# The opening of a two-layer model on one core: tokenizer bias as a product row, row copies on two engines, the first norm scaled on VectorE, a quarter turned inside the loop, constants loaded earlier

## The reference

```python
for i in range(9):                                  # tokenizer: dilated causal convolutions
    h = relu(conv1d(x, conv_w[i], dilation=2**i) + conv_b[i])
    x = x + h * scale[i] + shift[i]                 # batch norm folded into scale and shift
y = conv1d(x, out_w, 0, 1) + out_b                  # 4 -> 64 channels, one tap
h = transpose(y)                                    # (B, L, D)
xn = layernorm(h)                                   # no gain, no bias
q = einsum('btd,hrd->bhtr', xn, Q); k = einsum('bud,hrd->bhur', xn, K)   # 8 heads of rank 32
attn = softmax(q @ k.T / sqrt(64)); h = h + sum_h((attn @ xn) @ VO[h])
# then: a routed FFN of 8 experts, a second attention of another kind, a second FFN of 6 experts
```

## Time and profile before

| | us |
|---|---|
| median of 3 runs | 1347.37 |
| lowest and highest | 1346.24, 1347.96 |
| the profiled execution, its own time | 1345.62 |
| its span, first to last instruction | 1343.6 |

### The profile page before, as it was taken

The page is one execution under the profiler, slowest core; times in us unless marked ns, Lnnn a source line. Parts: engine busy times, 40 slices in busy tenths (PEclk is TensorE's granted clock), DMA queues, the critical chain, the costliest instruction groups (busy, mean ns, idle before and its releaser), DMA issues.

```text
span 1343.6 us, 27026 instructions
## 1 busy us (share of the span) xinstructions
PE 1228.2 (91%) x10203; PEld 785.8 (58%) x10203; DVE 780.1 (58%) x1724; ACT 641.1 (48%) x1372; POOL 526.5 (39%) x1110
## 2 busy tenths in 40 slices
PE   6889999999999999999999998699718888889998
PEld 5755565665666666666666665455415676676553
DVE  3545555665556566566566562142677898984542
ACT  1325555555554554554545544050245754744564
POOL 3211454754554644555455444405880120421200
PEclk8969999999999999999999999699858677568999
DMA  4100000000000000000000001012110000000001
GB/s 84 18 5 2 2 3 2 4 6 2 3 3 2 3 3 2 2 2 2 3 2 3 2 3 33 5 75 61 18 16 0 1 1 0 13 1 1 13 12 23
DMA packets 34076, 14.57 MB, mean 11 GB/s; under 512 B 30738, under 2 KB 31346, under 8 KB 33949
## 3 DMA queue, kind: packets, MB, share of 16 engines
q1 hardware_dynamic: 29341, 10.95, 3.6%
q0 software_dynamic: 4608, 1.91, 1.6%
HBM read 6.46 MB, written 7.27 MB: 10 GB/s over the span
## 4 chain that ended last, share of the span: by engine, by line
PE 73%; DVE 11%; POOL 5%; issue 5%; ACT 4%; SPq 2%; DMA 1%; POOLq 0%; DVEq 0%; ACTq 0%
PE psum L755 21%; PE psum L736 10%; PE psum L664 8%; PE psum L727 8%; PE psum L711 4%; POOL XN L1310 3%; PE psum L1008 2%; PE psum L649 2%; DVE arena L1978 2%; PE psum L558 2%; PE psum L988 1%; PE psum L669 1%; PE psum L809 1%; PE psum L822 1%; PE psum L1023 1%
## 5 line engine op out<-in xcount | busy, mean ns | idle before, releaser
L1428 ACT ACTIVATE arena<-psum 125x500 f32<-125x500 f32 x576 | 306.9, 585 | 337.7 <-PE psum L736 337.7
L1779 DVE TENSOR_REDUCE arena<-psum 125x1 f32<-125x500 f32 x384 | 242.4, 673 | 201.7 <-PE psum L664 201.7
L664 PE MATMUL psum<-arena 32*125 32x500 f32 (+1 forms) x1536 | 323.3, 517 | 0.6 <-ACT arena L1419 0.6
L755 PE MATMUL psum<-arena,XN 125*64 125x250 f32 x2304 | 307.9, 388 | 0.2 <-ACT arena L1428 0.2
L736 PE MATMUL psum<-arena 32*125 32x250 f32 x2304 | 291.7, 370 | 0.0
L736 PEld LDWEIGHTS psum<-arena 32*125 32x125 f32 x2304 | 214.6, 183 | 11.8 <-issue 1.0
L755 PEld LDWEIGHTS psum<-arena,XN 125*64 125x64 f32 x2304 | 140.3, 136 | 121.3 <-issue 78.6
L1782 DVE TENSOR_REDUCE arena<-psum 125x2 f32<-125x500 f32 x192 | 121.2, 673 | 71.7 <-PE psum L664 67.5
L664 PEld LDWEIGHTS psum<-arena 32*125 32x125 f32 x1536 | 126.8, 183 | 4.2 <-ACT arena L1419 1.2
L727 PE MATMUL psum<-arena,onesb 3*125 3x500 bf16 x576 | 122.4, 422 | 1.4 <-DMA arena<-arena 1.4
L1204 POOL TENSOR_TENSOR lnst<-lnst,mhalf 125x12 f32<-125x12 f32 x14 | 32.0, 2286 | 227.6 <-DVE lnst L1758 227.6
(11 more groups left out here) (342 smaller groups left out, 1970.9 us busy)
## 6 DMA issues: line engine op xcount, KB each, us to landing
arena<-arena SPq DMA_DIRECT2D x192, 1.5 KB
expert_in<-XN SPq DMA_DIRECT2D x8, 256.0 KB, 4.8
arena<-expert_in SPq DMA_DIRECT2D x4, 512.0 KB, 4.9
expert_out<-arena SPq DMA_DIRECT2D x4, 512.0 KB, 2.8
out<-H SPq DMA_DIRECT2D x16, 93.8 KB
expert_in<-XN,slot_in POOLq DMA_INDIRECT x48
XN<-expert_out,slot_out POOLq DMA_INDIRECT x48, 3.3
arena<-in_L_ffn_w SPq DMA_DIRECT2D x2, 256.0 KB
```

The source lines that it names most:

```text
L664: last = pe.matmul(ps[0:R, at_:at_ + hi - lo], QH[row:row + 32, b, g, j * R:(j + 1) * R], KH[row:row + 32, b, g, lo:hi], start=True, stop= ...
L755: last = pe.matmul(ctx_bank[64 * h2:64 * h2 + 64, 0:THIRD], XN[:, p, c, a, :], PR[:, x % 4, h2, i * THIRD:(i + 1) * THIRD], start=(c == 0) ...
L1428: act.activation(PR[:, x % 4, h2, :], st_bank[(2 * x + h2) % 3][0:R, 0:2 * THIRD], ACT.Exp)\
L1779: dve.reduce_max(MX[:, q % 2, 0, 2 * h2 + tile:2 * h2 + tile + 1], ps[0:R, 0:2 * THIRD], AX)\
```

## The change

- The output bias becomes row 96 of the product's weight, `Wout1`, loaded by a DMA that writes it 24 times into one partition; row 96 of `xc1` is set to 1 by GpSimd. The products have 97 rows.
- The six products are copied to `H` in one instruction each, the even ones by VectorE and the odd ones by ScalarE. ScalarE's two sines go behind its squares.
- VectorE clears `Fw`, as its first instruction. SP issues `prep` ahead of the eight zeroing DMAs; the `zeroed` counts are exchanged accordingly and `zeros` is cleared last.
- In the first norm GpSimd does the power alone, and VectorE the multiplication. VectorE's order is sum and centring of quarter 0, sum of quarter 1, variance 0, centring 1, variance 1, both scalings.
- Only quarter 0 is turned ahead of the attention. Quarter 1 becomes two ring jobs `("xt", 0, 1, h)` in steps 3 and 4, copied by VectorE; its `values_ready` follows them.
- The eight projections ahead of the loop go by halves of the rows; ScalarE copies Q, VectorE copies K.
- `busy`: 24 ahead of block 0 in place of 8; one after each score of `before`, and six after that list.

```diff
-        Wout, at = view(at, [NS * B, D], parts=96)
+        Wout1, at = view(at, [NS * B, D], parts=97)
+        Wout = Wout1[0:96]
...
-        xc, at = view(at, [SEG], parts=96)
+        xc1, at = view(at, [SEG], parts=97)
+        xc = xc1[0:96]
...
+            if x in (3, 4):
+                found.append(("xt", 0, 1, x - 3))
...
-        before = [job + (a,) for job in projections(0, 0) for a in range(2)]
+        before = [("proj", 0, 0, qk, th, a) for th in range(2) for qk in range(2) for a in range(2)]
...
+        halves = [(half, s) for half in range(2) for s in range(NS)]
...
-                busy(ps, 4 if i else 8)
+                busy(ps, 4 if i else 24)
...
-                    pe.matmul(ps[0:R, :], xc[:, half * R:(half + 1) * R], Wout[:, 8 * s:8 * s + 8, :],
+                    pe.matmul(ps[0:R, :], xc1[:, half * R:(half + 1) * R], Wout1[:, 8 * s:8 * s + 8, :],
...
-            for p in range(2):
-                transposes(0, xn_tile, p, S["normed0"], 6 if p else 34)
+            transposes(0, xn_tile, 0, S["normed0"], 34)
...
-                    if a == 0 and p >= 2:
-                        ring_emptied(pe, ("xt", 1, p, 0))
-                        ring_emptied(pe, ("xt", 1, p, 1))
+                    if a == 0 and p:
+                        for h in range(2):
+                            ring_emptied(pe, ("xt", int(p >= 2), p, h))
...
+                    if k_ == 0:
+                        pe.wait_ge(S["normed0"], 2)
...
-            ring_in(before)
+            for job in before:
+                ring(job)
+                if job[0] == "score":
+                    busy(st_bank[0], 1)
+            busy(st_bank[0], 6)
...
-            sp.dma_start(outb[:, :], t["L0_tok_out_b"].partition_broadcast(R)).then_inc(S["dma_conv"], 16)
+            sp.dma_start(Wout1[96:97], t["L0_tok_out_b"].unsqueeze(0).unsqueeze(0).to_broadcast([1, NS * B, D]))\
+                .then_inc(S["dma_conv"], 16)
 
             sp.wait_ge(S["zeroed"], 1)
+            for dst, src in prep:
+                sp.dma_start(dst, src).then_inc(S["dma_prep"], 16)
+            sp.wait_ge(S["zeroed"], 2)
             for e in range(E0):
...
-            sp.wait_ge(S["zeroed"], 2)
-            for dst, src in prep:
-                sp.dma_start(dst, src).then_inc(S["dma_prep"], 16)
...
+            pool.memset(xc1[96:97], 1.0)
...
-            pool.memset(Fw, 0.0)
...
-            scale(0, 0)
-            scale(0, 1)
+            for p in range(2):
+                pool.wait_ge(S["variance0"], p + 1)
+                pool.tensor_tensor(lnst[:, 3, p, :], lnst[:, 2, p, :], mhalf[0:R, 0:2 * NJ], ALU.pow)\
+                    .then_inc(S["rstd0"], 1)
...
+            for n, (half, s) in enumerate(halves):
+                if n % 2:
+                    ps, done = filled(act, ("h0", half, s))
+                    act.activation(H[:, :, 2 * s + half].rearrange("r p a d -> r a p d"),
+                                   ps[0:R, :].rearrange("r (a p d) -> r a p d", a=2, p=NP), ACT.Copy).then_inc(done, 1)
...
             for job in before:
-                if job[0] == "proj":
+                if job[0] == "proj" and job[3] == 0:
                     projected(job)
...
+            link(dve.memset(Fw, 0.0))
...
+                if n % 2 == 0:
                     ps, done = filled(dve, ("h0", half, s))
...
+                    dve.tensor_copy(H[:, :, 2 * s + half].rearrange("r p a d -> r a p d"),
+                                    ps[0:R, :].rearrange("r (a p d) -> r a p d", a=2, p=NP)).then_inc(done, 1)
...
+            def first_scale(p):
+                dve.wait_ge(S["rstd0"], p + 1)
+                dve.tensor_tensor(pairs(XN, p), pairs(XN, p), over(lnst[:, 3, p, :], 2 * NJ, D), ALU.mult)\
+                   .then_inc(S["normed0"], 1)
+
+            first_sum(0)
             dve.wait_ge(S["xbuf_zero"], 16 * E0)
...
+            first_centre(0)
+            first_sum(1)
+            variance(0, 0)
+            first_centre(1)
+            variance(0, 1)
+            first_scale(0)
+            first_scale(1)
...
+            for job in before:
+                if job[0] == "proj" and job[3] == 1:
+                    _, p, g, qk, th, a = job
+                    k = ring_at[job]
+                    dve.wait_ge(S["ring_full"], k + 1)
+                    dve.tensor_copy(KH[:, p + NP * a, g, th * HALF:(th + 1) * HALF], ring_bank[k % RB][:, 0:HALF])\
+                       .then_inc(ring_free[k % RB], 1)
```

More of the change, by code:

```diff
@@ L124, in build @@
         ppt, at = view(at, [NJ * R], parts=PP)
-        outb, at = view(at, [D], parts=R)
         phases, at = view(at, [NJ * PP + WN], parts=R)
@@ L249, in build @@
         sem(*[f"{what}{k}" for k in range(4) for what in ("centred", "squared", "variance", "normed")])
-        sem("dve_chain", "act_chain", "pool_chain")
+        sem("dve_chain", "act_chain", "pool_chain", "rstd0")
         sem("zeroed", "dma_conv", "dma_weights", "consts", "w96", "conv_w", "bn_var", "bn_rstd",
@@ L673, in ring @@
                     p = b % NP
-                    pe.wait_ge(S["lnb_done"], ln_at[(k_, b + NP if k_ == 1 else b)] + 1)
+                    if k_ == 0:
+                        pe.wait_ge(S["normed0"], 2)
+                    else:
+                        pe.wait_ge(S["lnb_done"], ln_at[(k_, b + NP if k_ == 1 else b)] + 1)
                     for i in range(3):
@@ L1181, in _ @@
             pool.memset(wearly, 0.0)
-            pool.memset(zeros, 0.0).then_inc(S["zeroed"], 1)
             pool.memset(qload, 0.0)
@@ L1185, in _ @@
             pool.memset(vox[:, :, :], 0.0).then_inc(S["zeroed"], 1)
+            pool.memset(zeros, 0.0).then_inc(S["zeroed"], 1)
             pool.wait_ge(S["consts"], 2)
@@ L1218, in _ @@
             link(pool.memset(SO[:, NJ, :], 0.0))
[L1219 to L1222, removed]
+            for h in range(2):
+                pool.wait_ge(full[jobs[("xt", 0, 0, h)] % 8], jobs[("xt", 0, 0, h)] // 8 + 1)
+            values_ready(0)
             for job in order:
@@ L1237, in _ @@
                     pool.tensor_scalar(nm[:, :, 2, :], rb, -1.0, None, ALU.mult).then_inc(S["shift_in"], 1)
-                elif kind == "xt" and job[1] == 1 and job[3] == 1:
+                elif kind == "xt" and job[1] < 2 and job[3] == 1:
                     pool.wait_ge(S["ring_full"], ring_at[job] + 1)
@@ L1360, in _ @@
                             ps, done = filled(act, ("qkp", qk, a))
-                            act.wait_ge(S["zeroed"], 2)
+                            act.wait_ge(S["zeroed"], 1)
                             act.activation(qkp[:, a, qk, :], ps[:, 0:256], ACT.Copy).then_inc(done, 1)
@@ L1409, in _ @@
             squares(0, 1, xn_flat(1))
+            act.wait_ge(S["trig_r"], 1)
+            act.activation(trig[:, 1, :], phases, ACT.Sin).then_inc(S["trig_done"], 1)
+            act.activation(trig[:, 0, :], trig[:, 0, :], ACT.Sin, bias=halfpi[0:R, :], scale=-1.0)\
+               .then_inc(S["trig_done"], 1)
             to_xt(0, 0)
-            to_xt(0, 1)
             def projected(job):
@@ L1735, in _ @@
                     dve.scalar_tensor_tensor(x1, x0, -1.0, x0, ALU.mult, ALU.max).then_inc(S["trig_r"], 1)
-            for half in range(2):
-                for s in range(NS):
+            for n, (half, s) in enumerate(halves):
+                if n % 2 == 0:
                     ps, done = filled(dve, ("h0", half, s))
[L1739 to L1745, removed]
+                    dve.tensor_copy(H[:, :, 2 * s + half].rearrange("r p a d -> r a p d"),
+                                    ps[0:R, :].rearrange("r (a p d) -> r a p d", a=2, p=NP)).then_inc(done, 1)
+            for half, s in halves:
+                emptied(dve, ("h0", half, s))
             def centre(k, p, src, dst):
@@ L1759, in variance, with first_sum, first_centre @@
                    .then_inc(S[f"variance{k}"], 1)
-            dve.wait_ge(S["xbuf_zero"], 16 * E0)
[L1762 to L1765, removed]
+            def first_sum(p):
+                link(dve.reduce_sum(lnst[:, 0, p, :], pairs(H, p), AX))
+                link(dve.tensor_scalar(lnst[:, 1, p, :], lnst[:, 0, p, :], -1.0 / D, None, ALU.mult))
+            def first_centre(p):
+                dve.tensor_tensor(pairs(XN, p), pairs(H, p), over(lnst[:, 1, p, :], 2 * NJ, D), ALU.add)\
+                   .then_inc(S["centred0"], 1)
+            def first_scale(p):
[3 more added lines that the diff above has]
+            first_sum(0)
+            dve.wait_ge(S["xbuf_zero"], 16 * E0)
+            first_centre(0)
[12 more added lines that the diff above has]
+                       .then_inc(ring_free[k % RB], 1)
             for job in order:
@@ L1796, in _ @@
                     p, a = b % NP, b // NP
-                    r = slice(0, 128) if which == 1 else slice(64 * a, 64 * a + 64)
+                    r = slice(0, 128) if which < 2 else slice(64 * a, 64 * a + 64)
```

## The result

The changed kernel takes 1355.7 us (median of six runs, 1354.9 to 1361.7) against 1347.7 before (six runs, 1346.2 to 1349.5): a ratio of 1.0071, 95% interval 1.0049 to 1.0092. It is slower by 0.7%, where 1335.7 was forecast with 1330.5 to 1344.0. Its profiled execution took 1355.9 (span 1353.6), 10.0 longer in the span than the one before.

The account below looks back on a forecast made before the run. The prediction took TensorE to bound the loop and one serial chain, with low clock in dense work, to bound what precedes it. Its terms summed to -11.7 us: 1335.7 against the median 1347.4, range 1330.5 to 1344.

Parts of the forecast that it names:

- Part 7: First score to loop: fillers part the paired scores, 1.1 us per score, 14.8 us instead of 10.30, +4.5.
- The clock falls in the scores: Rival: scores with filler take 2.2 us each at low clock, steps 0 to 2 their old 16.8; 1352, chance 0.15.
- Parts 1 and 2: Convolution blocks: longer filler starts block 0 at 16.4 us (+1.8); faster blocks, earlier constants, output product at 44.5 (-4.4).
- Part 3: Output product: bias as a row and copies split over two engines, -0.2 us.
- part 4: First norm, up to the first transposes: scaling on VectorE instead of GpSimd, -0.95 us.
- Part 5: First transposes to projections: the second quarter's turn no longer stands ahead of the projections, -3.8 us.
- Part 6: Projections to first score: full clock, K copied by VectorE beside ScalarE's Q, 3.4 us, -1.7.
- Part 9: Loop steps 3 and 4: six transposes enter where TensorE has no slack, +0.9 us.
- Part 8: Loop steps 0 to 2: 10.7 us instead of 16.8, -6.1, if the clock stays up.

Follow-up runs that it names:

- e4: Changed kernel with three fillers after each score instead of one; four runs 1349.3, 1349.6, 1369.1 and 1369.1 us, ratio 1.0111 to the kernel before.
- e3: Changed kernel with a filler after every second score only, the six behind the list kept; 1334.6 us, ratio 0.9913 to the kernel before.
- e1: Changed kernel without the twelve fillers after the scores and the six behind them; 1337.5 us, ratio 0.9929 to the kernel before.
- e7: e3 with the eight zeroing DMAs issued ahead of the constants again; 1338.1 us, ratio 0.9927 to the kernel before.
- e6: e3 with eight fillers ahead of block 0 instead of 24; 1331.6 us, ten runs from 1329.8 to 1344.9.
- e8: e3 with quarter 1 turned ahead of the attention again; 1333.1 us, ratio 0.9890 to the kernel before.
- e10: Kernel before with only a filler after every second score and six behind the list added; 1343.9 us, ratio 0.9966.
- e2: Kernel before with only a filler after each score and six behind the list added; 1364.3 us, ratio 1.0128.

## Why the prediction was wrong, point by point

**Part 7 failed, and with it the sign.** The prediction took 1.1 us a score at the high level and "+4.5"; measured is +22.7. Two things were wrong. The price at the high level is 1.42 to 1.45: a score alone takes 1.00 to 1.04, where twice 0.44 had been taken, the filler 0.23, and some 0.18 of changing over was left out (e4: two fillers more add 0.46, 0.115 a record, so the first one's 0.42 is not its own length). By e4 the stage would be 18.7 at the high level, +8.4. And the clock did not hold, which is the larger part: the other 14.2 of the 32.95, by the same estimate. Even at the high level parting the pairs loses more (8.4) than the clock gives back in steps 0 to 2 (5.5). e4 has no low microsecond from 14 us to the end of the attention and is no faster than the kernel before (1349.3 against 1346.9).

The rival "The clock falls in the scores" had the mechanism and its place right and got 0.15. It took 2.2 a score where 2.68 was measured and eight scores low where it was ten and part of an eleventh. It charged steps 0 to 2 their old 16.8, but they took 11.27, since the clock had risen at their start. So its 1352 lies near 1355.7 partly because these errors offset each other.

**The weighing that failed.** Against the rival I set the filler's 0.23 full-array microseconds in every 1.1. The row that I had at hand said more: at 77 to 80 us TensorE was printed busy 3.00 of 3.00 and the clock fell all the same: 0.59 at 80 to 82 us, and 0.50 at 88 to 90. In e3 the clock column shows 1.00 where the changed kernel shows 0.50, with the same twelve scores and half the fillers between them. It is not the number of fillers alone, since e4 with three a score held the clock in its profiled execution as well, nor the pairing alone, since the pairs of e1, with no filler, were followed by 0.50 from 70 us on. What in the parted stream lowers the clock stays open.

**Parts 1 and 2** were right in mechanism and 0.9 short: the first DMA landed at 7.21 instead of 7.59, and the filler ended at 15.7, not 16.4. e7 confirms the constants (+4.07 of wait). The long filler was not needed for the clock in e6's profiled execution, where the idle time before block 0 was 0.65 instead of 2.35. That those 2.35 had lost it in the kernel before is the likely reading; no run has the short filler with the long wait and the rest of the change.

**Part 3** gave about 0.1 for 0.2, **part 4** 0.76 for 0.95. GpSimd's two powers took 2.92 and 2.27 of the 5.19. The first began at 54.27, beside VectorE's two-input centring (54.10 to 55.05); I had put such a delay on the second, which began at 57.20, together with VectorE's two-input scaling, and was not delayed. The Trainium skill (SBUF — State Buffer, "Who interferes with whom") says that a two-input VectorE instruction contends with a GpSimd instruction that reads SBUF, and that one with at most one SBUF input, outside the two-port modes, does not. The first power's 2.92 and the memset's 3.66 agree; the second power's 2.27 shows that such a meeting need not cost anything.

**Part 5** was right in the profile (-3.8), but e8 shows that it isn't the move's worth: with the scaling off GpSimd, the second quarter costs 2.2, and 0.95 is paid in the loop. I had costed each edit against the kernel before, not against its neighbours.

**Part 6** gave 0.0 for 1.7: at 62 to 64 us the clock was 0.57. At the high level the stage is 3.76 to 3.78 (eight of the runs), so the size was right within 0.4 and the condition was not. What lowered the clock in the projections stays open.

**Part 9** was right: +0.95 for +0.9. **Part 8** was right in size, 11.27 for 10.7, and partly by luck: its condition, that the clock stays up, did not hold. The clock had been low for 30 us and was at 1.00 again from 98 us, just as the loop began. e3 comes out near the forecast (1334.6 against 1335.7), but this does not bear the forecast out: its score stage is 11.1 instead of 14.8, and part 6's 1.7 is missing there too.

**The rest**, 1119.0 against 1117.25, has the same code. In the fourteen profiled executions it lies between 1117.25 and 1122.5, so its +1.8 is within the spread of these kernels and no effect that the runs show. What sets it was not tried.

## What to carry to other kernels

A filler that keeps the clock up is not free beside matmuls that run side by side. If it takes the whole array, put it behind such a group and not within it (e10 gained 4 us, e2 lost 17), and count the changing over. A TensorE that is printed busy need not have the full clock: read the clock column over the stretch, and price such an edit at both levels. And cost each edit against the version without it, since two edits that free the same wait do not add.

## What the runs showed that I had not expected

- Two 32-row scores side by side take 1.04 us, one alone 1.00 to 1.04 at the high level; a full-array filler of 0.23 between two such matmuls costs 0.42. The Trainium skill (TensorEngine Tiling (Array Packing), "Key Properties") says that a change of tiling mode drains the engine; the 0.18 that is left over agrees, and nothing here parts the drain from the first filler's weight load.
- In the changed kernel the low level held for 30 us of work without a gap (68 to 98), past ten single fillers between scores, and ended with the fourteen filler records in a row (94.78 to 98).
- The Trainium skill (TensorE: Matmul & The Clock Gate, "What's actually happening") has the ratio set by how busy the engine has been. The printed busy time doesn't follow the clock here: 30.00 of 30.00 us at 0.50, 10.95 of 12.00 at 1.00 in e3.
- One kernel can have two times 20 us apart (e4: 1349.3 and 1369.1), with mean granted clocks of 0.922 and 0.907.
- At one clock level most stage lengths repeat to 0.1 us from kernel to kernel: steps 0 to 2 took 11.27 or 11.28 in nine of the fourteen.
